# Expert weights as the stationary operand, block steps reordered, and half of the weight squares on VectorE

## The reference

```python
# first block: layernorm, a gated recurrence over time, layernorm, residual
xp = x @ W_in.T ; gates = xp @ W_gate.T + b_gate      # i, f, o, c for 4 heads of 64
c  = sigmoid(f) * c + exp(i) * tanh(ct)               # scan over the 256 tokens
h  = sigmoid(o) * tanh(c * rsqrt(mean(c*c) + eps) * rms_w)
x  = x + layernorm(h @ W_out.T)
# second block: a mixture of 16 experts, 4 for each token
top_val, top_idx = top_k(layernorm(x) @ router.T + bias, 4)   # softmax over the four
gate, up = (xn @ gate_up_proj[e] + bias)[..., ::2], [..., 1::2]
out = ((clip(up) + 1) * (min(gate) * sigmoid(1.702 * gate))) @ down_proj[e] + bias
x  = x + layernorm(sum over the four experts of out * weight)
```

## Time and profile before

| | |
|---|---|
| runs | 798.18, 795.14, 796.6 us; median 796.6 us |
| profiled execution | 802.32 us; span 800.5 us; mean granted TensorE clock 0.859 |
| block steps, weights and routing | to about 371 us |
| tiles | 373 to 737 us |
| end | 737 to 800.5 us |
| busy in the span | PE 635.2, PEld 408.9, DVE 537.2, ACT 458.7, POOL 396.1 us |

### The profile page before, as it was taken

One profiled execution on the slowest core, in us unless ns is written; L12 is line 12 of the kernel. 1 busy time (PEld: TensorE's weight loads), 2 busy tenths in 40 slices (PEclk: granted clock), 3 DMA queues, 4 the chain that ended last, 5 costly groups with the idle time before them and its releaser, 6 DMA issues.

```text
span 800.5 us, 13282 instructions
## 1 busy us (share of the span) xinstructions
PE 635.2 (79%) x3658; PEld 408.9 (51%) x3658; DVE 537.2 (67%) x1570; ACT 458.7 (57%) x933; POOL 396.1 (49%) x300
## 2 busy tenths in 40 slices
PE   5887979598998752302999999999999999997450
PEld 2344636264565541201666666666666666664230
DVE  3637487778878978500777777777777777771892
ACT  2777686547546533101666767767767767762242
POOL 0012214654845737752466666666666656565121
PEclk9979798889989856555999999999999999997555
DMA  7966754799522223253677777776777676645987
GB/s 250 423 238 106 150 92 71 224 318 347 158 86 101 89 72 119 106 207 99 112 114 110 111 113 111 108 114 109 113 113 114 108 114 102 108 58 76 350 149 102
DMA packets 111895, 115.35 MB, mean 144 GB/s; under 512 B 31730, under 2 KB 101506, under 8 KB 110162
## 3 DMA queue, kind: packets, MB, share of 16 engines
q0 software_dynamic: 35456, 50.35, 37.2%
q1 hardware_dynamic: 76370, 64.16, 26.7%
HBM read 55.15 MB, written 59.31 MB: 143 GB/s over the span
## 4 chain that ended last, share of the span: by engine, by line
PE 59%; DVE 12%; DMA 8%; POOL 7%; ACT 6%; issue 5%; SPq 2%; POOLq 0%; ACTq 0%; DVEq 0%
PE PS L633 8%; PE PS L634 8%; PE PS L635 8%; PE PS L502 7%; POOL routed L916 6%; PE PS L624 4%; PE PS L653 4%; PE PS L641 4%; PE PS L654 4%; PE PS L655 4%; PE PS L525 2%; PE PS L533 2%; DMA W<-w_dn 2%; DMA W<-neg_mem 1%; DVE small L1325 1%
## 5 line engine op out<-in xcount | busy, mean ns | idle before, releaser
L942 POOL DMA_INDIRECT sums<-arena x144 | 223.2, 1550 | 143.8 <-ACT arena L702 71.5
L916 POOL DMA_INDIRECT routed<-arena,small x128 | 142.7, 1115 | 90.6 <-DVE small L1162 45.3
L1303 DVE TENSOR_SCALAR arena<-PS,small 128x256 f32<-128x256 f32 x144 | 78.3, 544 | 126.7 <-ACT arena L875 124.7
L702 ACT ACTIVATE arena<-PS 128x512 f16<-128x512 f16 (+1 forms) x180 | 105.1, 589 | 78.7 <-PE PS L624 45.7
L502 PE MATMUL PS<-arena 128*128 128x512 f32 x256 | 134.0, 668 | 10.7 <-ACT arena L702 10.6
L875 ACT ACTIVATE arena<-PS,small 128x256 f32<-128x256 f32 x144 | 68.1, 473 | 104.1 <-PE PS L635 104.1
L633 PE MATMUL PS<-W,arena 128*128 x288 | 110.2, 382 | 0.0
L634 PE MATMUL PS<-W,arena 128*128 x288 | 110.1, 382 | 0.0
L635 PE MATMUL PS<-W,arena 128*128 x288 | 109.9, 382 | 0.0
L502 PEld LDWEIGHTS PS<-arena 128*128 128x128 f32 x256 | 51.9, 214 | 69.3 <-issue 65.8
L624 PE MATMUL PS<-ident,arena 128*128 128x128 f16 x576 | 56.3, 221 | 36.7 <-DMA arena<-routed 35.9
(11 more groups left out here) (164 smaller groups left out, 1023.3 us busy)
## 6 DMA issues: line engine op xcount, KB each, us to landing
arena<-routed SPq DMA_DIRECT2D x144, 128.0 KB
W<-w_gu SPq DMA_DIRECT2D x8, 1024.0 KB, 23.6
W<-neg_mem POOLq DMA_DIRECT2D x16, 512.0 KB, 8.5
sums<-zero SPq DMA_DIRECT2D x2, 4096.0 KB, 26.2
W<-sums SPq DMA_DIRECT2D x16, 512.0 KB, 8.8
X<-x SPq DMA_DIRECT2D x8, 512.0 KB, 4.8
W<-w_dn SPq DMA_DIRECT2D x4, 1024.0 KB, 11.4
out<-X SPq DMA_DIRECT2D x8, 512.0 KB, 3.0
```

Of the source, the lines that this page charges most:

```text
L702: return nc.scalar.activation(o, i, ACT.Copy, **kw)
L916: pool.indirect_dma_start(routed, bass.IndirectOffsetOnAxis(ap=idx, axis=0), rows[b][:, jk // TOPK, :], None).then_inc(rows_sent[lane], 16)
L942: pool.indirect_dma_start(sums[j % SUMS], bass.IndirectOffsetOnAxis(ap=dst[j % MU], axis=0), yb[u], None, compute_op=ALU.add).then_inc(y_s ...
L1303: L.send(v.tensor_scalar(up[j % 2], acc[:, FF:2 * FF], gu_hi, gu_lo, ALU.min, ALU.max))
```

## The change

In the tiles:

- `gate_up` swaps the operands. For each of four groups of 128 hidden columns and both halves of the inputs, a 128x128 piece of the weights is the stationary operand and `xq` moves, 128 columns: 24 products with 24 weight loads of 128x128, in place of 6 and 6. Its result is already transposed (hidden columns on the partitions).
- `act_transposes` goes away, with its semaphore; ACT's `ah` and DVE's `a_low` read `act_` from SBUF.
- The lags go from 3 and 4 to 2 and 3. `gate_up` waits for `act_ready` as well. The transposed rows have two PSUM banks.

In the steps: 12 of the 24 squares go to DVE (`squares_v`: four in step 0, six in step 1, two in step 2), the other 12 stay on ACT, in steps 0 to 2. On PE the mean square, the transposes for it, its spread and the output product come later in step 1, and the spread and the transposes of x2 come one chunk later in all steps. `evac_x` waits for the gate products in two halves. `row_high` moves from the last chunk of a step to the first of the next.

```diff
-A_LAG, D_LAG = 3, 4
+A_LAG, D_LAG = 2, 3
-CONV_DN = ((1, 4), (1, 6), (2, 2), (2, 4), (2, 6), (3, 2), (3, 4), (3, 6))
+CONV_DN = ((1, 4), (2, 0), (2, 2), (2, 4), (2, 6), (3, 2), (3, 4), (3, 6))
-SQUARE_AT = (((0, 4),) * 2 + ((0, 5),) * 2 + ((0, 6),) * 2 + ((0, 7),) * 2
-             + ((1, 2), (1, 3), (1, 3), (1, 5), (1, 5), (1, 7), (1, 7))
-             + ((2, 0),) + ((2, 4),) * 3 + ((2, 5),) + ((3, 0),) + ((3, 4),) * 3)
+SQUARE_ACT = {(0, 6): (0,), (0, 7): (2, 4, 6), (1, 1): (8,), (1, 2): (10,), (1, 3): (12,), (1, 5): (14,), (1, 6): (16,),
+              (1, 7): (18,), (2, 1): (20,), (2, 3): (22,)}
...
-        xT16 = PS[:, 3, 0:DIM].bitcast(f16)
+        xT16 = [PS[:, 3 + b, 0:DIM].bitcast(f16) for b in range(2)]
...
+                    if c == CHUNKS - 1 and k == 0:
+                        last.then_inc(gate_half, 1)
...
-                    if c == 1 and mid:
+                    if c == (3 if s == 1 else 1) and mid:
                         mean_square(s - 1)
...
-                    if c == 3 and mid:
+                    if c == (6 if s == 1 else 4) and mid:
                         rms_spread(s - 1)
-                    if c == 3 and old:
+                    if c == 4 and old:
                         transposes_x2(s - 2)
...
-                if j >= 1:
-                    pe.wait_ge(xq_ready, j)
+                if j >= 2:
+                    pe.wait_ge(xq_ready, j - 1)
...
             def gate_up(j, e):
                 acc = PS[:, j % 3, :]
                 pe.wait_ge(xq_ready, j + 1)
+                if j >= 3:
+                    pe.wait_ge(act_ready, j - 2)
                 w = W16[:, ds(e * (2 * PART) + GU0 * 2 * PART, 2 * PART)]
-                for k in range(KT):
-                    hi, lo = [w[:, h * PART + k * 2 * FF:h * PART + (k + 1) * 2 * FF] for h in range(2)]
-                    mm(acc, xq[j % NX][:, k, :], hi, start=(k == 0), stop=False)
-                    mm(acc, xq[j % NX][:, k, :], lo, start=False, stop=False)
-                    last = mm(acc, xq[j % NX][:, KT + k, :], hi, start=False, stop=(k == KT - 1))
+                for f in range(2 * FF // P):
+                    part = acc[:, f * P:(f + 1) * P]
+                    for k in range(KT):
+                        hi, lo = [w[:, h * PART + k * 2 * FF + f * P:h * PART + k * 2 * FF + (f + 1) * P] for h in range(2)]
+                        mm(part, hi, xq[j % NX][:, k, :], start=(k == 0), stop=False)
+                        mm(part, hi, xq[j % NX][:, KT + k, :], start=False, stop=False)
+                        last = mm(part, lo, xq[j % NX][:, k, :], start=False, stop=(k == KT - 1))
                 last.then_inc(gu_mm, 1)
...
-                if 0 <= j - A_LAG < TILES:
-                    act_transposes(j - A_LAG)
...
+                    if t >= 2:
+                        act.wait_ge(y2_mm, t - 1)
+                    act.wait_ge(act_ready, t + 1)
+                    copy(ah[t % 2], act_[t % NB].rearrange("p (k t) -> p k t", k=KT),
...
+            def squares_v(count):
+                for _ in range(count):
+                    n = odd[0]
+                    odd[0] += 2
+                    c = order(n)
+                    if n == 1:
+                        dve.wait_ge(s_down, 16 * PARTS_DN // 2)
...
+                    v.scalar_tensor_tensor(junk_v, source(c), 1.0, source(c), ALU.mult, ALU.mult,
+                                           accum_out=ssq[:, c:c + 1]).then_inc(squared_v, 1)
...
+                if s == 0:
+                    squares_v(PARTS_DN // 2)
...
                     hidden(s - 1)
+                    squares_v((0, 3, 2)[s] if s < 3 else 0)
```

More of the change, by code:

```diff
@@ L208, in build @@
         x2 = x2_own[:, :].rearrange("p (j d) -> p j d", j=BT)
-        junk = W16[:, GU0 * 2 * PART:GU0 * 2 * PART + PART].bitcast(bf16)
+        junk, junk_v = [W16[:, GU0 * 2 * PART + h * PART:GU0 * 2 * PART + (h + 1) * PART].bitcast(bf16) for h in range(2)]
         at[0] = 0
@@ L584, in step @@
                         peaks(s // 4)
-                    if c == 3 and mid:
+                    if c == (5 if s == 1 else 3) and mid:
                         rms_transpose(s - 1)
-                    if c == 3 and mid:
+                    if c == (6 if s == 1 else 4) and mid:
                         rms_spread(s - 1)
-                    if c == 3 and old:
+                    if c == 4 and old:
                         transposes_x2(s - 2)
-                    if c == 4 and old:
                         logits(s - 2)
-                    if c == 4 and mid:
+                    if c == (7 if s == 1 else 4) and mid:
                         out_product(s - 1)
@@ L620, in row_transposes @@
                 pe.wait_ge(x_in[j % UN], 16 * (j // UN + 1))
-                if j >= 1:
-                    pe.wait_ge(xq_ready, j)
+                if j >= 2:
+                    pe.wait_ge(xq_ready, j - 1)
                 for k in range(2 * KT):
-                    last = nc.tensor.transpose(xT16[:, k * P:(k + 1) * P], xrow[j % UN][:, k * P:(k + 1) * P], ident16[:, :])
+                    last = nc.tensor.transpose(xT16[j % 2][:, k * P:(k + 1) * P], xrow[j % UN][:, k * P:(k + 1) * P], ident16[:, :])
                 last.then_inc(x_mm, 1)
@@ L711, in evac_x @@
                     act.wait_ge(xT_mm, 2 * t + (k + 1))
+                    if t and k == 0:
+                        act.wait_ge(gate_half, t)
+                    if t and k == KT - 1:
+                        act.wait_ge(gate_mm, 8 * t)
                     copy(xT[:, k, :], PS[:, k, :]).then_inc(xT_ready, 1)
@@ L788, in squares @@
                     act.wait_ge(s_down, 16 * PARTS_DN // 2)
-                if c < PARTS_GU and c % 2 == 0:
+                if c < PARTS_GU:
                     act.wait_ge(s_moe[c // 2], 16)
-                act.wait_ge(squared, n + 1)
+                if n:
+                    act.wait_ge(squared, n // 2)
                 nc.scalar.activation(junk, source(c), ACT.Square, accum_out=ssq[:, c:c + 1]).then_inc(squared, 1)
@@ L807, in weight_work @@
             def weight_work(s, c):
-                for n, at in enumerate(SQUARE_AT):
-                    if at == (s, c):
-                        squares(n)
+                for n in SQUARE_ACT.get((s, c), ()):
+                    squares(n)
                 for n, at in enumerate(CONV_DN + CONV_GU):
@@ L819, in step @@
                         evac_x2(s - 2)
-                    if c == 4 and mid:
+                    if c == 4 and mid and s > 1:
                         tanh_c(s - 1)
@@ L828, in step @@
                         gate_chunk(s, c)
-                    if c == CHUNKS - 1 and mid:
+                    if s == 1 and c == CHUNKS - 1:
+                        tanh_c(0)
+                    if s == 2 and c == 1:
+                        norm_y(0)
+                    if c == CHUNKS - 1 and mid and s > 1:
                         norm_y(s - 1)
-                    if c == CHUNKS - 1 and old:
+                    if c == CHUNKS - 1 and s == NBLK + 1:
                         row_high(s - 2)
+                    if c == 0 and on(s, 3):
+                        row_high(s - 3)
                     if c == 1 and on(s, -1):
@@ L1168, in peak_row @@
                 lo, hi = ((0, PARTS_GU), (PARTS_GU, PARTS))[which]
-                dve.wait_ge(squared, 1 + (PARTS_DN if which else PARTS))
+                dve.wait_ge(squared, (PARTS_DN if which else PARTS) // 2)
+                dve.wait_ge(squared_v, (PARTS_DN if which else PARTS) // 2)
                 L(v.tensor_reduce(peak, ssq[:, lo:hi], AX, ALU.max))
@@ L1247, in step @@
                         slots(s - 3)
+                    if s == 1:
+                        squares_v(1)
                     hidden(s - 1)
+                    squares_v((0, 3, 2)[s] if s < 3 else 0)
                 if s == 8:
@@ L1292, in a_low @@
                 dve.wait_ge(ah_ready, j + 1)
-                v.scalar_tensor_tensor(al[j % 2], PS[:, 4 + j % 2, 0:FF].rearrange("p (k t) -> p k t", k=KT),
+                v.scalar_tensor_tensor(al[j % 2], act_[j % NB].rearrange("p (k t) -> p k t", k=KT),
                                        act_scale, ah[j % 2], ALU.mult, ALU.subtract).then_inc(al_ready, 1)
```

28 lines of the change are left out of this document (12 added, 16 removed).

## The result

| | before | after |
|---|---|---|
| runs | 795.14, 796.6, 798.18, 800.53 us | 911.74, 914.6, 916.57, 916.69 us |
| median | 797.39 us | 915.59 us |
| ratio | | 1.147, 95% interval 1.1416 to 1.1524 |
| profiled execution, span | 802.32, 800.5 us | 914.6, 912.8 us |
| first row transposes start | 373.6 us | 398.1 us |

A forecast was written before the change was run, and what follows sets the result against it. PE bounds the kernel; in the changed tiles its sequencer would. Profiled 802.3 - 10 (steps) + 79 (tiles) - 5 (end) = 866.3, less 5.7 to the median 860.6, set at 859 us; own range 836 to 884, wider range 828 to 905.

The forecast's parts named there:

- Rival 2: Tiles: 98 ns weight loads stand in full ahead of each product, +118 us, 900 us in all; chance 0.06.
- The failed step: Steps: moved PE parts, `row_high` and `evac_x` halves change order and no work; 0, with 5 us either way.
- Steps, the rest: Block steps: squares shared between ACT and DVE shorten the chain; -10 us (-20 to +5).
- the square of the cell: Start of step 1: on ACT it would come at about 40.7 instead of 44.5, -3.8 us.
- The wait for X in step 4: Steps: with all squares done in step 2, this wait of 2.9 us goes.
- DVE's further squares: Steps: 8 further squares (10.2 us) lie where DVE waits; cost nothing, +10 if that cover is gone.
- Tiles: Expert tiles: PE's sequencer becomes the bound, 2.95 us a tile against 2.40, over 144 tiles +79 us (+45 to +95).
- The count (23 operations and the table): A tile on PE's sequencer: 20 addresses and 3 waits at 0.125 us, plus 0.07 for expert table loads, 2.95 us.
- End of the stage: After the last tiles: POOL has no backlog of transfers, only the last three tiles bunched; -5 us (-6.4 to 0).
- Profile to median: Whole kernel: the profiled execution lies 5.7 us above the runs' median, so -5.7, then 2 towards the bounds' middle.
- Rival 1: Tiles: register operations shared between products, so addresses don't bind and the kernel gets faster, 776 us; chance 0.14.
- Rival 3: Tiles: the waiting array's clock drops to 1.2 GHz, for a third of the tiles +69 us, 928 us; chance 0.06.

The follow-up runs named there:

- h0_steps: The changed block steps with the tiles of the kernel before: 824.4 us, ratio 1.0323 to the kernel before.
- h3_both_back: Changed steps, tiles of before, with step 1's order and the later place of spread and x2 transposes both undone: 791.81 us, ratio 0.9919 to before.
- f4_both_rowhigh_back: As h3_both_back, with `row_high` also back in the last chunk of a step: 793.0 us, ratio 0.99 to the kernel before.
- e2_tiles: The changed tiles with the block steps of the kernel before: 885.28 us, ratio 1.1123 to the kernel before.
- e3_static: As e2_tiles, but `gate_up` always takes expert 0's weights at a fixed address: 796.12 us, ratio 0.9983 to the kernel before.
- e5_moving_split: The kernel before, with each `gate_up` product of 512 moving weight columns cut into four of 128: 876.58 us, ratio 1.0969 to before.

## Why the prediction was wrong

The direction and the mechanism in the tiles were right; the time, 915.6 us, lies 10.6 us above the range and 31.6 above 884, the end of the forecast's own range. The upper end of 905 rests on the second rival's 900 us, and that rival is out; the lower end, by the terms as written, would be 827 and not 828. By the forecast's own steps, in profiled executions (sum 866.3, measured 914.6):

- **The failed step: "The moved PE parts, `row_high` and the halves of `evac_x` I put at 0, with 5 us either way: they change the order and no work."** The moved parts cost 32.6 us (h0_steps against h3_both_back). An order adds no work, but it decides what covers a wait, and here also at which clock the work is done. I had priced each edit of the steps by what it adds, and had not asked of each move what stood between a producer and its reader. Between the spread and the logits it was a gate chunk, which covered DVE's slots; in the trace of before the logits follow it without a gap. The lower clock then made what stood behind the wait 1.5 and 1.7 times as long (2.77 against 1.85 us, 6.25 against 3.70). In step 1 the term names PE's parts only; the change moves ACT's tanh, the row of the mean square and the norm of y as well, and I had not priced them at all. In the timelines it is the tanh on which DVE and then PE wait. `row_high` at 0 was right within some 4 us (f4_both_rowhigh_back).
- **Steps, the rest: -10.** Measured with the moves undone: -7.5, within what I gave, and near it in part by luck: the square of the cell came at 42.75, not 40.7, which is 1.75 us gained of 3.8. DVE was done at 40.64, as I had worked out; I had left out that ACT, too, has an order, with three squares of its own in that place. The wait for X in step 4 is gone, as forecast. That DVE's further squares cost nothing is not shown by itself; with the moves undone the whole is a gain.
- **Tiles: +79 (bounds +45 to +95); measured +93.3**, and +88.4 for the whole kernel e2_tiles, in which the end gives some 6 us back. The count (23 operations and the table) was right, the size of one was not: the 124 ns that most distances show are the usual value, not the mean. About one in six register operations comes 138 to 279 ns behind the last one, and the mean distance in the tiles is 0.1315 us: 23 x 0.1315 + 0.07 = 3.09, against 3.098 measured. In the trace of before the same mean is 0.133 already, so it could have been read there. The tile of before, 2.45 over the whole stage and not 2.40 as in the one I read, took 7 us off again.
- **End of the stage: -5; measured -5.5.**
- **Profile to median: -5.7 and 2 more towards the middle of the bounds.** Neither held: the profile of the changed kernel lies 1.0 below its median. Together 8.3 of the miss of 56.6; the steps are 34.5, the tiles 14.3, the end -0.5.
- **Rival 1** (addresses don't bind) is out in the changed kernel: L636 and L638 have sixteen operations. Its pace was right where they are taken away: e3_static has 2.42 a tile, and POOL waits for landings again. So even without the sixteen addresses the swap buys nothing here, beside POOL's transfers.
- **Rival 2** (loads unhidden): out, by e3_static's 0.055. The rule of the Trainium skill, "TensorE: Matmul & The Clock Gate", section "Back-to-back issue gap", of about 81 ns for a product of 128 columns with its load, isn't borne out either: twenty-four took 0.055 to 0.056 each.
- **Rival 3** (clock at 1.2 GHz in the tiles): out, 0.98 from 400 to 500 us. A lower clock came where I had not looked for it, in the steps: 0.80 against 0.85 from 60 to 300 us.

## What to carry to other kernels

Count the operands whose address is data, not the products: each different piece cost 0.13 us of PE's sequencer here, with products of 128, 256 and 512 columns alike, and cutting those of 512 into four turned some hidden 1.3 us a tile into a bound of 3.1. A move in a hand-written order is priced like an added wait: write down for each moved part who produces its input, who reads its output, and which piece of work stood between them. Undo moves together as well as singly, for they need not add up.

## What the runs showed that I had not expected

- The register operations' price hardly depends on which operand is addressed (e5_moving_split 3.006 us with two waits, e2_tiles 3.10 with three), and falls away with a fixed address (no operation for those products in e3_static).
- The clock fell in the changed steps right behind a stretch in which PE was busy for 5.0 of 7.7 us at the full clock, and cost more than the wait of 1.55 us: 6.25 against 3.70 us for the same 16 products. Before, a low stretch exists as well (0.71 from 222 to 230 us), but it falls on the spread, the transposes and a gate chunk, which grow by less than 1 us each.
- Five kernels with the steps of before reached the first row transposes at 365.5 (e2_tiles), 366.3, 371.3, 373.6 and 374.0 us in their profiles: a difference below 8 us in that stage between two single profiles says nothing by itself.
